# Waiting for each indirect transfer of GpSimd to land, in a macaron model with mixture-of-experts layers

## The reference

```python
x = x + 0.5 * ffn(layernorm(x))      # MoE step 0 in layer 0, step 2 in layer 1; ffn adds its own input
x = x + attention(layernorm(x))
x = x + 0.5 * ffn(layernorm(x))      # MoE step 1 in layer 0, step 3 in layer 1
```

## Time and profile before

| | us |
|---|---|
| median of 3 runs | 762.65 (761.97 to 771.69) |
| span of the profiled execution | 751.7 |
| TensorE busy | 616.4 |
| VectorE busy | 404.3 |
| GpSimd busy | 318.2 |
| ScalarE busy | 263.8 |

### The profile page before, as it was taken

The page is one execution under the profiler, slowest core; times in us unless marked ns, Lnnn a source line. Parts: engine busy times, 40 slices in busy tenths (PEclk is TensorE's granted clock), DMA queues, the critical chain, the costliest instruction groups (busy, mean ns, idle before and its releaser), DMA issues.

```text
span 751.7 us, 15429 instructions
## 1 busy us (share of the span) xinstructions
PE 616.4 (82%) x4590; PEld 567.3 (75%) x4590; DVE 404.3 (54%) x1385; ACT 263.8 (35%) x549; POOL 318.2 (42%) x352
## 2 busy tenths in 40 slices
PE   2597888959969598767879779798898989888987
PEld 1386777848759488667779779697887979877987
DVE  6744343815528146342445335297796876954446
ACT  2233342523524333322333223443634435323331
POOL 4535444261441633544350534514615736344134
PEclk9999899989989989786988889899999999998999
DMA  7578576635626347564765657475564575556853
GB/s 253 149 221 260 170 204 212 194 110 148 187 75 199 116 143 222 155 208 135 216 197 149 190 156 214 136 207 164 173 201 132 159 232 156 181 166 224 261 157 76
DMA packets 113268, 133.57 MB, mean 178 GB/s; under 512 B 10931, under 2 KB 76227, under 8 KB 112806
## 3 DMA queue, kind: packets, MB, share of 16 engines
q1 hardware_dynamic: 104998, 115.79, 52.6%
q0 software_dynamic: 8192, 16.79, 7.4%
HBM read 103.83 MB, written 28.71 MB: 176 GB/s over the span
## 4 chain that ended last, share of the span: by engine, by line
PE 59%; DVE 12%; another core or an unknown queue 12%; issue 7%; ACT 7%; POOL 2%; DMA 0%; DVEq 0%; ACTq 0%
PE up_gate L1029 18%; PE up_gate L1022 11%; PE y L983 10%; PE side L1110 3%; PE y L985 3%; PE side L1044 2%; ACT hidden L581 2%; POOL b_rstd L486 2%; PE side L1060 2%; DVE hidden L686 2%; PE side L1126 2%; ACT x_res L598 2%; DVE rms_out L708 1%; DVE kv_lo L872 1%
## 5 line engine op out<-in xcount | busy, mean ns | idle before, releaser
L686 DVE TENSOR_TENSOR hidden<-up_gate,hidden 128x256 f32<-128x256 f32 (+1 forms) x240 | 115.7, 488 | 252.0 <-ACT hidden L581 125.0
L1029 PE MATMUL up_gate<-rows_T,up 128*128 128x128 f32 x1440 | 194.5, 286 | 26.0 <-issue 14.0
L1029 PEld LDWEIGHTS up_gate<-rows_T,up 128*128 128x128 f32 x1440 | 181.4, 200 | 32.4 <-issue 19.6
L495 POOL DMA_INDIRECT rows_dram<-rms_out,rows_of x128 | 130.1, 1016 | 171.8 <-DVE rows_of L832 90.5
L581 ACT ACTIVATE hidden<-up_gate 128x256 f32<-128x256 f32 (+1 forms) x240 | 104.3, 436 | 279.8 <-PE up_gate L1022 103.0
L514 POOL DMA_INDIRECT y_rows<-y_dram,rows_of x120 | 121.9, 1016 | 85.3 <-ACT hidden L581 46.1
L1022 PE MATMUL up_gate<-rows_T,up 128*128 128x128 f32 x960 | 139.7, 291 | 16.5 <-ACT rows_T L586 9.6
L1022 PEld LDWEIGHTS up_gate<-rows_T,up 128*128 128x128 f32 x960 | 126.7, 203 | 24.7 <-issue 22.1
L983 PE MATMUL y<-down,hidden 128*128 x480 | 78.7, 288 | 8.2 <-DVE hidden L686 6.0
L486 POOL TENSOR_TENSOR b_rstd<-b_var,minus_half 128x8 f32<-128x8 f32 x16 | 26.8, 1674 | 121.6 <-DVE b_var L703 121.5
L983 PE MATMUL y<-down_a,hidden 128*128 x480 | 76.3, 283 | 0.0
(11 more groups left out here) (188 smaller groups left out, 700.4 us busy)
## 6 DMA issues: line engine op xcount, KB each, us to landing
up<-in_up SPq DMA_DIRECT2D x120, 352.0 KB
up<-in_up SPq DMA_DIRECT2D x120, 256.0 KB
rows<-rows_dram SPq DMA_DIRECT2D x47, 256.0 KB, 3.0
y_dram<-y_tile SPq DMA_DIRECT2D x45, 256.0 KB, 2.5
rows_dram<-zeros SPq DMA_DIRECT2D x12, 256.0 KB, 3.6
rows<-rows_dram SPq DMA_DIRECT2D x16, 192.0 KB
y_dram<-y_tile SPq DMA_DIRECT2D x15, 192.0 KB
rows_dram<-rms_out,rows_of POOLq DMA_INDIRECT x128
```

The source lines that it names most:

```text
L495: pool.indirect_dma_start(out=xg_d[g], out_offset=bass.IndirectOffsetOnAxis(ap=pos[g][:, at:at + 1], axis=0), in_=xs(Z, GROUPS[g][c // TB] ...
L686: dve.tensor_tensor(h, u, h, ALU.mult).then_inc(mult_done, 1)
L1029: last = pe.matmul(U[q % 3][:, c * P:(c + 1) * P], upW[n % RING][:, at + c * P:at + (c + 1) * P], rows_, start=True, stop=True)
```

## The change

The wait `pace` (GpSimd goes ahead with a pair of transfers of slot t only when `silu` of tile t − 2 is done) is taken out. In its place GpSimd remembers the semaphore and the count that its last indirect transfer reaches on landing, and waits for it before it issues the next one. The scatters, the gathers and the early gathers are all treated so. Nothing else is changed: the order of the work and all other waits stay.

```diff
-            def pace(t):
-
-                if 1 < t <= SLOTS:
-                    pool.wait_ge(silu_done, t - 1)
+            landing = []
+
+            def landed_when(sem, count):
+
+                landing[:] = [(sem, count)]
+
+            def wait_landed():
+
+                for sem, count in landing:
+                    pool.wait_ge(sem, count)
...
-                    pace(t)
                     for at in (2 * c, 2 * c + 1):
+                        wait_landed()
                         pool.indirect_dma_start(out=xg_d[g], out_offset=bass.IndirectOffsetOnAxis(ap=pos[g][:, at:at + 1], axis=0),
...
+                        landed_when(scattered[g], 16 * (2 * CH[g] * (turns(s1, g) - 1) + at + 1))
...
-                    pace(t)
...
                         at = 2 * i + k2
+                        wait_landed()
                         pool.indirect_dma_start(out=gath[b % 2][:, (TB * k2 + c) * P:(TB * k2 + c + 1) * P], out_offset=None,
...
+                        landed_when(gathered[b][c // 2], 16 * (TB * s + 2 * (c % 2) + k2 + 1))
...
                     at = 2 * c + k2
+                    wait_landed()
                     pool.indirect_dma_start(out=gath[b % 2][:, (TB * k2 + c) * P:(TB * k2 + c + 1) * P], out_offset=None,
...
+                    landed_when(gathered[b][c // 2], 16 * (TB * s + 2 * (c % 2) + k2 + 1))
```

## The result

The changed kernel takes 1136.55 us (median; 1131.7 to 1138.04) against 762.31 us for the kernel before in the same group of runs, a ratio of 1.487 with a 95% interval of 1.479 to 1.495. The profiled execution took 1135.75 us and its span is 1134.0 us.

A forecast was written before the change was run, and what follows sets the result against it. GpSimd's serial queue was to bound the changed kernel: 256 transfers × 3.5 = 896 us plus gaps it can't fill (19.6, 4.7, 55, 0, 13, 70, 6) make 1064 us of span, with 10.9 us more 1075 us; range 940 to 1210.

The forecast's parts named there:

- all these are satisfied: Pace waits on GpSimd, 46.1 + 39.9 us before, are always met once GpSimd is late; removing them is worth 0.
- the pitch: Time from one indirect transfer's issue on GpSimd to the next: 3.5 us, for 256 transfers 896 us.
- 2.25 − 0.4 + 0.8 = 2.7 us in quiet: Unloaded transfer: issue to SyncE's load, less the waiting engine's reaction, plus landing to next issue.
- straight line in the DMA share: Time per transfer between 2.7 us in quiet and 5.5 us under 85% load; 3.7 us at 42% share.
- the way into steps 2 to 3: GpSimd's gap from the half combine, needing four of eight gathers, to the first gather: 27.1 − 14 = 13 us.
- the serial gaps: GpSimd idle time awaiting its own last output: 55 us in steps 0 to 1, 70 us in steps 2 to 3.
- what lies around the span: Median of the runs over the profiled span: 10.9 us before, the same added to the new 1064 us.
- The periods: Foreseen lengths: 70 us in steps 0 to 1, 56 in steps 1 to 2, 73 in steps 2 to 3.
- A pitch always quiet: Rival: transfers stay below 3.0 us each as the stalled machine leaves the DMA engines alone; 870 to 947 us, chance 0.13.
- The congested case: Rival: loaded landings or a throttled TensorE; at 4.0 us per transfer 1203 us, perhaps some tens more; chance 0.10.
- Covered: Rival: slack between batches hides the 17.6 us that each batch grows; time stays 763 us; chance 0.02.
- faster: Rival: in steps 2 to 3 transfers stay below 1.94 us each, so dropping the pace gains 20 us, 743 us; chance 0.01.

The follow-up runs named there:

- the costs of the two kinds: The changed kernel with the landing wait before scatters alone, 886.37 us, or before gathers alone, 917.57 us, beside 646.84 us for the kernel before.
- the runs above: The changed kernel; with up weight loads cut to 64 columns, 1067.3 us; with the wait before scatters alone, 886.37 us; before gathers alone, 917.57 us.

## Why the prediction held, and where its terms were off

**Right: the bound and the direction.** "GpSimd becomes the chain" is shown by the 61% of the chain in indirect transfers, by 1142 us with a before of 646, and by the costs of the two kinds adding up. The removed pace is worth nothing (646.75 for 646.38), and the waits themselves fold away (646.42). The reason given for the pace's 0, "all these are satisfied", holds only in part: put back, it was waited for 21 times (88.8 us), at the longest places where GpSimd stood as long without it.

**Too small: the pitch, by 49 us.** I took 3.5 us. All gaps taken out, the 256 transfers fill 945 us, 3.69 each. Two errors stood against each other in the term. The step "2.25 − 0.4 + 0.8 = 2.7 us in quiet" took off the 0.4 us between the last packet and SyncE's instruction, as if GpSimd could go ahead at the last packet. It can't: SyncE issues 2.28 us after the last scatter (825.37 to 827.65 below), just as in the earlier trace rows, GpSimd's own wait is over after 2.24 us, and its next transfer in quiet comes at 3.0 us. The chain in order of time (start, us, what) splits the pitch: 2.24 us of transfer, 0.03 and 0.71 us of the register move and the preparation, and 3.54 us of transfer in a loaded one:

```profile
222.81 3.54 DMA rows_dram<-rms_out,rows_of
...
227.11 2.24 DMA rows_dram<-rms_out,rows_of
229.38 0.03 POOLq L501
229.41 0.71 issue
230.12 2.92 DMA rows_dram<-rms_out,rows_of
```

So it is 2.25 + 0.75 for a scatter in quiet, with nothing to take off; a quiet gather takes 3.3 us, and no row of the prediction gave it a price of its own. The other error went the other way. The prediction's straight line in the DMA share rises by 0.41 us for each 10% of share, where the runs above give some 0.15; with the 0.4 us put back it would have given some 4.0 us at the 40% measured, too much. Most landings are quiet ones, as I had argued: 51% of the scatters inside batches follow within 3.2 us, 53% of the gathers within 3.5. In the last 19 us of a batch of gathers no other engine works, and the DMA engines are 8% busy:

```profile
257.00:276.00 19.00, 0.00 (x0) 0.00 (x0) 0.00 (x0) 0.00 (x0) 7.35 (x7) 0.50 0.08 21
```

The two errors nearly cancel, and that the term came out within 0.2 us is in part luck. The scatter that SyncE waits for, and its load of rows:

```profile
825.37 0.99 POOL L501 DMA_INDIRECT rows_dram<-rms_out,rows_of  x1 [2.04 <-DMA rows_dram<-rms_out,rows_of]
```

```profile
827.65 0.38 SPq L386 DMA_DIRECT2D rows<-rows_dram  x1
```

**Missed: the products behind the gathers, 17 us.** For the way into steps 2 to 3 I wrote 13 us, from the half combine's four gathers. The gap is 30 us. The first attention of layer 1 has its four products in GpSimd's queue behind eight gathers, and VectorE stood 26 us for them before it came to that combine:

```profile
737.00 4.14 POOL L557 TENSOR_TENSOR attention<-attention 128x512 f32<-128x512 f32 x4
```

```profile
738.77 2.92 DVE L882 TENSOR_TENSOR kv_lo<-attention,kv_hi 128x512 fp32r<-128x512 f32 x1 [26.14 <-ACT kv_hi L649]
741.62 0.60 DVE L732 SCALAR_TENSOR_TENSOR x_res<-y_rows,w_first,x_res 128x128 f32<-128x128 f32 x2
```

The fourth gather, the last that this half combine needs, was issued at 721.33; that VectorE came to it only at 741.62 is the wait for the products. I had named them in the queue and then costed the wrong waiter. No run moves the products, so this is read from the trace alone.

**Nearly right: the serial gaps.** The gaps from the last gather's landing to the next scatter in steps 0 to 1 are 14 to 18 us each over the usual reissue, 65 us for my 55: from `b_rstd`'s end to the scatter 18.5 us (276.04 to 294.55) for 14.5 in the earlier trace rows. In that work TensorE had a granted clock of 0.68, for 1.00 in the same place before. No run sets the clock by itself, but the same trace has this way twice with 91 matmuls recorded: in the period before, at a granted clock of 0.82, it took 15.9 us with TensorE 12.75 us busy, here 18.5 us with 15.54 us. So the slower matmuls account for the difference between these two periods. Before both, TensorE had stood still through the end of the batch of gathers, with a granted clock of 0.50, its lower level (1.2 GHz); and the prediction's "every stall lets the clock fall" says too much, since the first window of the earlier trace rows, 2.3 us with TensorE half idle, has 1.00. The four gaps of steps 2 to 3 sum to 63 us for my 70, the first one to 3.9 for 4.7, the end to 5 for 6. The clock in those stretches, two of after and one of before:

```profile
203.70:219.60 15.90, 12.75 (x91) 11.56 (x92) 13.28 (x60) 5.67 (x12) 1.01 (x2) 0.82 0.31 86
276.00:294.50 18.50, 15.54 (x91) 14.49 (x92) 13.44 (x60) 5.71 (x12) 1.04 (x2) 0.68 0.26 77
```

```profile
132.10:147.50 15.40, 14.85 (x122) 13.34 (x121) 12.99 (x58) 7.58 (x17) 2.68 (x2) 1.00 0.69 202
```

**Wrong but small: what lies around the span.** I took 10.9 us from a median and a span of different executions. An execution's own time is 1.75 us over its span here (1135.75 and 1134.0). So the span was 70 us too small, and the time 61.5: 49 (pitch) + 17 (products) + 10 − 7 − 1 − 1 + 2 of small gaps = 69, less 9 us around it.

**The periods.** Foreseen 70, 56 and 73 us; the first scatters of the groups lie 71 to 76 us apart in steps 0 to 1 and 57 to 63 in steps 1 to 2, the first gathers 73 to 77 in steps 2 to 3. With 16 × 3.69 = 59 us and gaps of 16 us this is twice a batch plus the gap, as the prediction asked, and the mean pitch is between its 3 and 4 us; single transfers follow after 3.0 to 7.4 us. TensorE's busy time rose to 638 us, its share fell to 56%, the mean clock to 0.785.

**The rivals.** A pitch always quiet (870 to 947) fell: the mean is 3.69 with a quiet one of 3.0 to 3.3. The rule that was set beside it, 2.0 us and the bytes (the Trainium skill, "DMA: Bandwidth & Descriptors", Anatomy of one DMA), gives 2.15 us; here a quiet scatter lands after 2.24 us and a quiet gather after some 2.55, and the fit has no term for the load. The congested case (1203) was nearer than the quiet one: the result lies about halfway between the forecast and it. "Covered" and "faster" fell outright.

## What to carry to other kernels

Here a wait for each transfer's landing turned a queue that issues one every 1.3 us into one that issues one every 3.7, and everything else in that queue waited along. In such a case add up the queue as if it were the whole kernel, with the gaps that it can't fill. Take the pitch from the issue to the moment when a waiter is let go, plus the preparation of the next transfer, and subtract nothing that wasn't seen at such a waiter. When a queue grows late, go through each item in it and look for who waits for it; the one that I missed was four small products that took 4 us themselves and cost 17. Two transfers in flight gave 370 of 495 us back where the kernel before takes 646 us.

## What the runs showed of the hardware that I had not expected

- The same kernel took 646 us in three groups of runs and 758 to 762 in two, with a granted clock of 0.98 and 0.93, and in the slower case TensorE was held in stretches that I found no record to explain. The transfers weren't slower there: back to back they went at 1.3 us in both. The cause is open.
- A wait in front of an indirect transfer is free when it is met (1.3 us from one to the next), but when it isn't, the next transfer begins 0.75 us later than SyncE's would in the same place.
- With two in flight many transfers pair up, 1.3 us and then 2.5 to 4 us; the mean is 2.2 us for scatters and 2.1 for gathers, and not half of 3.7.
- The mean pitch behind a landing grows slowly with the load: 3.34, 3.63 and 3.81 us for scatters at DMA shares of 22, 40 and 52%.
